# Top-k read without a select pass and without row statistics in its loop; the statistics of 12 batches move to the second cross-attention

## What is computed

```
def top_k_read(query, mem, top_k=32, Wq, bq, Wk, bk, Wv, bv, Wo, bo):   # first block
    q = query @ Wq.T + bq;  k = mem @ Wk.T + bk;  v = mem @ Wv.T + bv
    scores = einsum('btd,bsd->bts', q, k) / sqrt(d)
    keep the 32 largest of the 1601 scores of each row, all others -inf
    attn = softmax(scores);  return (attn @ v) @ Wo.T + bo

def heads_read(q, k, v, norm_w, norm_b, ...):                            # fourth block
    qn = layernorm(q, norm_w, norm_b);  kn = layernorm(k, ...);  vn = layernorm(v, ...)
    Q, K, V = projections of qn, kn, vn into 16 heads of 16
    A = softmax(Q K^T / 4);  O = A V + Q
    return layernorm(O, norm1_w, norm1_b) @ Wo + bo + O

x = x + top_k_read(layernorm(x), ctx, 32, ...)
x = x + retention(layernorm(x), ...)
x = x + mha_and_experts(layernorm(x), ...)
x = x + heads_read(layernorm(x), ctx, ctx, ...)
```

## Time and profile before

| | us |
|---|---|
| median of 3 runs | 1661.69 |
| lowest, highest | 1656.72, 1661.87 |
| the profiled execution | 1658.01 |
| its span | 1656.2 |

### The profile page before, as it was taken

The page is one execution under the profiler, slowest core; times in us unless marked ns, Lnnn a source line. Parts: engine busy times, 40 slices in busy tenths (PEclk is TensorE's granted clock), DMA queues, the critical chain, the costliest instruction groups (busy, mean ns, idle before and its releaser), DMA issues. The chain is left out here.

```text
span 1656.2 us, 29794 instructions
## 1 busy us (share of the span) xinstructions
PE 1468.4 (89%) x11472; PEld 1147.0 (69%) x11472; DVE 994.2 (60%) x1896; ACT 652.8 (39%) x1266; POOL 640.2 (39%) x558
## 2 busy tenths in 40 slices
PE   6988877765993899999999999999999994789998
PEld 3645645444893688888888888888888873456676
DVE  4999954476237456666666665666566643464444
ACT  1444432131201455555555555555455431322322
POOL 0000000001002557877767877677876531311100
PEclk9777788867996999999999999999899965899999
DMA  9479700800322666676676675676674531220000
GB/s 357 145 281 323 264 0 1 296 1 0 104 101 88 172 167 153 163 195 164 153 162 155 159 187 150 157 166 148 164 188 101 112 66 51 80 102 0 1 1 26
DMA packets 109296, 219.61 MB, mean 133 GB/s; under 512 B 10871, under 2 KB 83095, under 8 KB 108391
## 3 DMA queue, kind: packets, MB, share of 16 engines
q1 hardware_dynamic: 109163, 217.80, 47.0%
HBM read 132.51 MB, written 6.40 MB: 84 GB/s over the span
## 5 line engine op out<-in xcount | busy, mean ns | idle before, releaser
L1905 DVE TENSOR_REDUCE d_top<-psum 128x1 f32<-128x400 f32 (+2 forms) x512 | 270.4, 570 | 97.6 <-PE psum L1549 90.4
L1449 POOL TENSOR_TENSOR d_ring<-d_ring 128x512 f32<-128x512 f32 x224 | 289.8, 1294 | 77.0 <-ACT d_ring L1734 59.4
L1734 ACT ACTIVATE d_ring<-psum 128x512 f32<-128x512 f32 (+1 forms) x416 | 229.3, 595 | 206.2 <-PE psum L1567 187.2
L1567 PEld LDWEIGHTS psum<-d_queries,d_stack 100*128 100x128 f32 (+1 forms) x1664 | 214.3, 198 | 36.3 <-issue 33.7
L1567 PE MATMUL psum<-d_queries,d_stack 100*128 100x128 f32 (+1 forms) x1664 | 235.4, 286 | 1.2 <-DVE d_queries L1920 0.9
L1549 PE MATMUL psum<-d_stack,d_queries 96*128 96x400 f32 (+1 forms) x512 | 171.6, 393 | 13.4 <-DVE d_top L1905 10.6
L1379 POOL TENSOR_TENSOR d_rowsT<-d_raw,d_rowsT 128x768 fp32r<-128x768 f32 (+2 forms) x62 | 117.9, 1903 | 154.0 <-ACT d_rowsT L1705 154.0
L1534 PE MATMUL psum<-d_wv,d_rowsT 128*128 128x256 f32 (+1 forms) x1248 | 170.4, 286 | 0.0
L1526 PE MATMUL psum<-d_rowsT,d_wk 128*128 128x384 f32 (+2 forms) x768 | 160.3, 358 | 3.6 <-POOL d_rowsT L1379 1.9
L1534 PEld LDWEIGHTS psum<-d_wv,d_rowsT 128*128 128x128 f32 (+1 forms) x1248 | 161.9, 187 | 0.5 <-issue 0.5
L973 POOL TENSOR_TENSOR c_partL<-moe_in,c_partH 128x256 fp32r<-128x256 f32 x8 | 5.5, 730 | 388.5 <-ACT c_partH L1061 388.5
(11 more groups left out here) (393 smaller groups left out, 2303.0 us busy)
## 6 DMA issues: line engine op xcount, KB each, us to landing
d_stack<-d_stage SPq DMA_DIRECT2D x384, 200.2 KB, 4.2
a_cR<-ctx_rows_dram SPq DMA_DIRECT2D x16, 1664.0 KB, 9.5
a_cT<-ctxT_dram SPq DMA_DIRECT2D x16, 1601.0 KB, 14.5
moe_w<-moe_w_dram SPq DMA_DIRECT2D x16, 1024.0 KB, 11.3
d_rowstd<-row_stds_dram SPq DMA_DIRECT2D x16, 801.0 KB, 5.7
d_raw<-ctxT_dram SPq DMA_DIRECT2D x32, 384.0 KB, 5.7
d_raw<-ctxT_dram SPq DMA_DIRECT2D x16, 512.0 KB, 6.3
d_queries<-queries_dram SPq DMA_DIRECT2D x96, 64.0 KB, 2.0
```

The source lines that it names most:

```text
L1449: pool.tensor_tensor(sums[:, 0, m, :], first, ring[:, slot_of(u, m, c), :], ALU.add)\
L1567: last = pe.matmul(ps[0:w, S_BANK + (m + c) % 2, j * P:(j + 1) * P], stack[0:STACKED, m, j, c * P:c * P + w], queries[0:STACKED, m, j, :], ...
L1734: act.activation(ring[0:w, slot_of(u, m, c), :], ps[0:w, S_BANK + (m + c) % 2, :], ACT.Exp)\
L1905: dve.tensor_reduce(top[:, m, v:v + 1], ps[:, M_BANK + v % 2, 0:min(w, S - s0)], X, ALU.max)\
```

## The change

**In the read.** `TILE` runs through the tiles from 7 down to 0. Tile 7 of x is loaded, normalised and projected first, and the first scores start by quarters of `a_cT`; the other tiles follow in two sets (3 to 6, 0 to 2), in between the first scores. The loops are unrolled. DVE's `choose` has the search alone. ACT takes the exponential of `left` too (what was chosen gives 0), and POOL subtracts: probabilities = exp(scores) - exp(left). The total is the sum over the exponentials of the 32 values found, on ACT. `left`, `probs` and `best` are doubled. For the last tile DVE subtracts. The bias is added to x on POOL at the start. The output projection of tiles 4 to 7 stands before the last two tiles' values. A context row r is now on partition r // 13 (13 rows in one piece per partition, 124 partitions used), so the probabilities are turned from columns 13 apart.

**Row statistics.** None in the loop. `a_cR` still holds batches 0 to 3 at its end: batches 2 and 3 are taken by DVE at the end of the read, 0 and 1 between retention's copies, which stores the four batches' result itself. The other 12 are taken in the second cross-attention: while batch b runs, SP loads the rows of batch b + 4 in two halves into `d_room` (where parameter packs pd1 and, at the end, pd2 lie), DVE takes the statistics in groups 5 and 6 of each half and five small operations at the batch's end, ACT takes Ln and Exp(-0.5 x) in the next batch, and SP stores and loads them again for the rows of that batch.

The core of the diff:

```diff
         @block.gpsimd
         def _(pool):
-            pool.memset(cstats[:, :, :], 0.0).then_inc(sig("a_cleared"), 1)
...
+            for n in range(LAST):
+                pool.wait_ge(sig("a_exp"), n + 1)
+                pool.wait_ge(sig("a_gone"), n + 1)
+                pool.tensor_tensor(probs[:, n % 2, 0:S], probs[:, n % 2, 0:S], left[:, n % 2, :], ALU.subtract)\
+                    .then_inc(sig("a_probs"), 1)
...
# PE
-            score(0, 0, first=True)
-            score(0, 1)
-            value(0, 0, first=True)
-            with pe.Fori(1, NT // 2) as i:
-                score(i, 0)
-                value(i - 1, 1)
-                score(i, 1)
-                value(i, 0)
-            value(NT // 2 - 1, 1)
...
+            turn(2, 4, xn, "a_xnT")
+            score(0)
+            for g in (1, 2):
...
+                project(g, 6, core.w("l0_wqT"), xnT, "a_qT")
...
+                project(g, 4, core.w("l0_wk"), qT, "a_keyqT")
+                bias(g)
+                if g == 1:
+                    score(1)
+            for n in range(1, LAST):
+                score(n + 1)
+                turn_probs(n - 1)
+                value(n - 1)
...
# ACT
+            for n in range(1, NT):
+                exp_left(n - 1)
+                if n >= 2:
+                    take_read(n - 2)
...
+                    gather(n + 1)
+                exp_scores(n)
...
+                take_probs(n - 1)
...
# DVE
-                dve.scalar_tensor_tensor(probs[:, :], left[:, :], LOWEST, probs[:, :], ALU.is_le, ALU.mult,
-                                         accum_out=total[:, u:u + 1]).then_inc(sig("a_probs"), 1)
...
-                    choose(ci, cu)
-                    row_stats(ci, cu)
...
+            for n in range(NT):
+                choose(n)
...
+            row_stats(dve, cR, cstats, 2).then_inc(sig("a_row_stats"), 1)
...
# retention
+            row_stats(dve, cR, cstats, 0, range(0, 9))
...
+                if i < 3:
+                    last = row_stats(dve, cR, cstats, 0, range(9 + 6 * i, min(15 + 6 * i, 2 * NC)))
...
# second cross-attention
+    CONTEXT_AT = {5: (0, 1, 2, 3), 6: (4, 5, 6)}
...
+            def load_context(b, h):
+
+                done = 2 * (b - RESIDENT) + h
...
+                wait(sp, "d_row_stats", done)
+                cs = HALVES_OF[h]
+                sp.dma_start(rows_in[:, 0:cs.stop - cs.start, :],
+                             drams["ctx_rows"][bass.ds(b, 1)].rearrange("b (p c) d -> p (b c) d", c=NC)[:, cs, :])\
+                  .then_inc(sig("d_context_in"), 16)
...
+                act.activation(row_std[:, :], row_var[:, :], ACT.Ln).then_inc(sig("d_row_ln"), 1)
+                act.wait_ge(sig("d_row_ln"), done + 1)
+                act.activation(row_std[:, :], row_std[:, :], ACT.Exp, scale=-0.5).then_inc(sig("d_row_std"), 1)
...
+                    if i in CONTEXT_AT.get(g, ()):
+                        if i == 0:
+                            dve.wait_ge(sig("d_context_in"), 16 * (2 * done + h + 1))
...
+                        last = dve.bn_stats(row_moments[:, c, :], rows_in[:, i, :])
```

More of the change, by code:

```diff
@@ L368, in score @@
+            def score(n):
+                t, u = TILE[n], n % 2
+                projected(pe, "keyqT", set_of(t))
+                if n:
+                    for j in range(2):
+                        pe.wait_ge(sig(f"a_cT_in{u}{j}"), 16 * (n // 2 + u))
                 for c, (s0, w) in enumerate(QUARTERS):
+                    if n:
+                        pe.wait_ge(sig("a_scores"), 4 * (n - 1) + c + 1)
+                    else:
+                        pe.wait_ge(sig(f"a_quarter_in{c}"), 32)
@@ L375, in score @@
                     last.then_inc(sig("a_scores_ps"), 1)
-                if not first:
-                    pe.wait_ge(sig("a_means"), 5 * n)
-                for j in range(2):
-                    for c in range(SHARE):
-                        for k in range(KD):
-                            last = pe.matmul(ps[:, SUM_BANK, j * SHARE + c:j * SHARE + c + 1],
-                                             cT[:, u, j, k, c * P:(c + 1) * P], ones[:, :], start=(k == 0),
-                                             stop=(k == KD - 1))
@@ new lines, in _ @@
+            pe.wait_ge(sig("ident_in"), 16)
+            pe.wait_ge(sig("a_ln_out"), 1)
+            turn(0, 4, xn, "a_xnT")
+            pe.wait_ge(sig("a_pa0_in"), 16)
+            for s, v in both(sig, "a_xnT", 1):
+                pe.wait_ge(s, v)
+            project(0, 6, core.w("l0_wqT"), xnT, "a_qT")
+            projected(pe, "qT", 0)
+            project(0, 4, core.w("l0_wk"), qT, "a_keyqT")
+            bias(0)
+            pe.wait_ge(sig("a_ln_out"), 1 + len(SETS[1]))
+            pe.wait_ge(sig("a_qbk"), 1)
@@ new lines, in _ @@
+            for part, tiles in enumerate((slice(FIRST, NT), slice(0, FIRST))):
+                act.wait_ge(sig("a_var"), part + 1)
+                act.activation(std[:, tiles], var[:, tiles], ACT.Sqrt).then_inc(sig("a_std"), 1)
+                if part == 0:
+                    take(0, 0, 4, xnT, "a_xnT")
+                    act.wait_ge(sig("a_pa0_in"), 16)
+                    take(0, 0, 6, qT, "a_qT", core.p("l0_bq"))
+                    take(0, 0, 4, keyqT, "a_keyqT")
+                    take_bias(0)
@@ new lines, in _ @@
+            take(1, 0, 6, xnT, "a_xnT")
+            take(2, 0, 4, xnT, "a_xnT")
+            gather(0)
+            for k in range(KD):
+                take(1, k, 6, qT, "a_qT", core.p("l0_bq"))
+            exp_scores(0)
+            for k in range(KD):
+                take(1, k, 4, keyqT, "a_keyqT")
+            take_bias(1)
+            for k in range(KD):
+                take(2, k, 6, qT, "a_qT", core.p("l0_bq"))
+            gather(1)
+            for k in range(KD):
+                take(2, k, 4, keyqT, "a_keyqT")
@@ new lines, in _, with row_stats @@
+            dve.tensor_copy(readT[:, 1, 0:HALF], ps[:, 3, :]).then_inc(sig("a_readT_d"), 1)
+            dve.wait_ge(sig("a_valT_ps"), 4)
+            dve.tensor_scalar(valT[:, 1, 0:HALF], ps[:, 5, :], core.p("l0_bv")[:, 1:2], None, ALU.add)\
+               .then_inc(sig("a_valT_d"), 1)
+            for i in range(2, 4):
+                add_out(i, i)
+def row_stats(dve, cR, cstats, first, chunks=range(2 * NC)):
+    for i in chunks:
+        b, c = first + i // NC, i % NC
+        last = dve.bn_stats(cstats[:, b * NC + c, :], cR[:, (NT - 1 - b // 2) % 2, b % 2, c, :])
+    return last
```

628 lines of the change are left out of this document (371 added, 257 removed).

## The result

| kernel | median (lowest to highest), us | runs |
|---|---|---|
| before | 1659.2 (1654.8 to 1661.9) | 4 |
| changed | 1700.8 (1698.9 to 1704.5) | 4 |

The ratio is 1.026, with a 95% interval from 1.023 to 1.029. The forecast was 1601 us with a range from 1580 to 1626; it has the wrong sign. All times here are medians of the fast executions, so one slow execution of experiment 6 (1665.2 us) and one of experiment 7 (1641.1 us) are left out. The profiled execution has a span of 1697.1 us, against 1656.2.

What follows compares the result with a forecast made beforehand. VectorE was taken to bound the read, PE the second cross-attention. The terms -63.7 + 1.5 + 4 = -58.2 gave 1599.8 us from the profiled 1658.0, 1603.5 from the median; 1601 was said, range 1580 to 1626.

Steps and rivals of the forecast that it cites:

- the read: Top-k read: VectorE no longer bounds, tiles follow at 18.45 us, end at 190.5 instead of 254.2 us: minus 63.7.
- Retention: Retention phase: statistics of batches 0 and 1 fit into VectorE's waits, a store ends the phase: plus 1.5 us (0 to 5).
- Second cross-attention ... five small operations (about 1 us) ... plus 4 (0 to 15): Second cross-attention: statistics, small operations, half loads and store for twelve batches, about 0.35 us each: plus 4 us.
- the prediction weighed two others: Read: skill rules of 358 GB/s HBM (18.7 us of transfers a tile) and 16-byte lines (some 3 us more a tile).
- the low part at 855.59: Second cross-attention: VectorE's copy that PE needs at 857.57; seven statistics leave it in time, six and small operations 0.2 us late.
- The slower case: Second cross-attention: VectorE's wait for the half context holds adds and low parts, PE waits; at 3 us a half 1672; 5%.
- The transfer rival: Read: all transfers at 349 GB/s, 19.1 us a tile, read ends at 208, total 1618 us; 6%.
- The clock rivals: Read: slow PE clock, 20.9 us a tile, 1618 us (15%); or fast PE, value 5.8 us, 1588 us (15%).
- Heads cost 1 us a half: Second cross-attention: each half of a batch costs 1 us, 24 us more, total 1622 us; 8%.
- One sign of being wrong: Second cross-attention: the forecast is wrong if that phase takes over 15 us more.
- The one beside it: Heads loop: the forecast is wrong if PE's waits for d_stage or d_stack sum to more than 10 us.
- the signs of being right: Value's ends 18.5 us apart, GpSimd's subtraction near 4, cR at 400 GB/s or more, L2191 without long wait, PE 51.4 of 52.

Runs made afterwards that it cites:

- experiment 6: Changed kernel without the 13 statistics a batch and the half loads in the second cross-attention, small operations kept: 1637.8 us.
- experiment 7: Changed kernel with the five small operations made by GpSimd, at the end of group 1 of the next batch: 1609.9 us.
- experiment 8: Changed kernel with the small operations on VectorE where GpSimd is idle (next batch's second half, end of group 0), statistics double-buffered: 1620.1 us.
- experiment 5: Changed kernel without the five small operations of a batch, Ln reading one column of the statistics directly: 1618.7 us.
- experiment 11: Changed kernel with small operations on VectorE where GpSimd is idle, and five of seven statistics a half one group earlier: 1606.7 us.
- experiment 10: Changed kernel with small operations on GpSimd (end of group 1, next batch) and five of seven statistics a half one group earlier: 1603.4 us.
- experiment 4: Changed kernel without statistics, small operations, Ln, Exp and store in the second cross-attention, half loads kept: 1607.2 us.
- experiment 12: Changed kernel with small operations on GpSimd in its idle stretch (next batch's second half), five of seven statistics a half one group earlier: 1603.1 us.
- 9: Changed kernel with only GpSimd's scaling of raw rows moved, from groups 0, 1, 2 of the first half to 2, 3, 4: 1637.3 us.

## Why the prediction was wrong

**The read and the retention phase: right in the main.** The forecast was -63.7 for the read; measured -57.9. On PE the end of each tile's value (L451) tells where the 5.8 us arose. The first ends at 65.31 us, forecast 60.2. The first search starts at 26.04 (forecast 22.3) and the second at 46.05 (40.4); PE came to score(0) at 19.49 in place of 16.2, having waited 4.61 us for VectorE's normalising of the other seven tiles. The sixth ends at 157.45, forecast 152.5. So the five tiles between took 18.43 us each, and 18.45 was forecast. The pace was right, but not every term of it: three of the tiles take 17.0 to 17.2 us on PE, and the two in which PE waits for cT (3.0 and 2.0 us) take 20.2 and 20.8. VectorE's searches follow each other faster, in 16.7 us in the mean from 46.05 to 146.53, because the first of them started with PE's scores already ahead. The eighth value ends at 184.67 (forecast 183), and the projection and sum behind it take 11.7 us where 7.5 was forecast. Retention: +1.8, forecast +1.5. The phases behind it up to 467 us, forecast 0, cost 3.7 us more; 2.1 of these are one group of 32 matmuls (L221, before L219), which takes 16.09 us at a granted clock of 0.87 in place of 13.97 at 1.00. Where the rest arises was not looked for.

**The step that failed: "Second cross-attention ... five small operations (about 1 us) ... plus 4 (0 to 15)".** It measured 93 us by the spans. Two things were wrong in it.

First the size. "About 1 us" stood there without a row. It is what the five take where GpSimd is idle (0.9 us a batch in experiment 8). They took 53.5 us in 12 batches, 4.5 each time, since operations on VectorE waited for GpSimd's running instruction. The trace of before had such durations, in rows that the forecast read as plain work: one addition of 512 columns takes 0.68 us in one place and 1.67 in another, and three take 2.28 us at 851.72 and 3.26 at the next half's end. The minimum, median and maximum over all 128 say it in one line:

```profile
L1934 DVE TENSOR_TENSOR d_ring<-d_ring x128: 679/692/2127, 586.3 to 1372.2; 128x512 f32<-128x512 f32 x96, 65x512 f32<-65x512 f32 x32
```

```profile
832.18 1.67 DVE L1934 TENSOR_TENSOR d_ring<-d_ring 128x512 f32<-128x512 f32 x1
...
875.49 3.26 DVE L1934 TENSOR_TENSOR d_ring<-d_ring 128x512 f32<-128x512 f32 x3
```

The bounds that the forecast should have had stand in that row: five operations between 5 x 0.17 and 5 x (2.13 - 0.69), so 0.9 to 7 us a batch, up to 86 us in all (an estimate from that row).

The Trainium skill states the mechanism (its page "SBUF — State Buffer", section "Who interferes with whom"): a VectorE instruction with two inputs in SBUF contends with a GpSimd instruction that reads SBUF, and the one that comes second is blocked until the other ends. This case's trace agrees: 1.71 us beside GpSimd's 1.69, 0.17 where GpSimd is idle. By the same section an instruction with at most one such input, outside the modes that use both ports, is spared; the statistics, one input, take 402 to 428 ns in all 156 cases, beside GpSimd or not. The reader who wants a rule that spoke against this change would have found it there; the prediction weighed two others.

Second the wait. The forecast asked when the low part at 855.59 was due. PE needs something earlier: the denominators, which wait for the addition of chunk 12. On the timeline of PE before, at a half's end and at a batch's end:

```profile
856.07 0.62 PE L1595 MATMUL psum<-d_ring,d_ones 128*32 128x128 f32 x16
...
879.85 0.62 PE L1595 MATMUL psum<-d_ring,d_ones 128*32 128x128 f32 x16
```

The additions were done at 854.00 and 878.75: 2.07 us of slack in the middle of a batch and 1.10 at its end. The seven statistics of the first half nearly fit (in the changed kernel PE waits there in the first batch only, 0.93 us). Six statistics and small operations were put at the end with 1.10. So even at 1 us for the five, part of the 3.0 us would have been late; experiment 5, without the small operations, shows that part: 11 us, and 13 come back when the statistics are moved (experiment 11 against 8).

**Waits and clock.** From the first statistics of the second cross-attention to the end PE runs the same 9170 matmuls in both kernels, so the stretch splits by its busy time (columns as in the earlier trace rows; before, then changed):

```profile
519.65:1656.20 1136.55, 1065.84 (x9170) 856.99 (x9170) 660.55 (x1177) 512.22 (x907) 633.28 (x544) 0.93 0.50 125
467.26:1697.10 1229.84, 1100.01 (x9170) 881.99 (x9170) 758.38 (x1393) 519.85 (x931) 621.46 (x544) 0.90 0.51 132
```

PE is idle for 70.7 us before and for 129.8 now: 59.1 of the 93.3 us. The other 34.2 are the same matmuls taking longer, at a granted clock of 0.90 in place of 0.93: after the wait shown above PE works at the lower level for some microseconds, and the same eight score matmuls take 1.97 us at 646.13, behind a wait of 5.50. Experiment 8 has all the work and takes 79.2 us less from that point on, 49.3 of idle time and 29.9 of matmuls. So each microsecond of idle time came with about 0.6 of slower matmuls. The granted clock over the whole span is 0.890 in the changed kernel, 0.914 in experiment 8, 0.923 in the fastest run of experiment 10.

**The rivals.** The slower case had the right sign, and PE did stand behind VectorE's adds, but for another reason: L2191 never waits for the half load, and experiment 4 prices the loads at 8 us. The transfer rival is refuted for the read (433 GB/s). The clock rivals did not come either: PE's clock was 0.84 to 1.00 in the tiles, above the 0.76 and 0.81 of before. "Heads cost 1 us a half" put 24 us on this phase, a quarter of what it cost. With the small operations and the statistics in better places the kernel takes 1603 us. That this is near the 1601 forecast is in part luck: in the profile of experiment 10 the second cross-attention starts 50.4 us earlier than before, where 62.2 was forecast, and what comes from there on takes 9.4 us less, where 4 more was forecast.

**The signs named in advance.** One sign of being wrong came true: the phase takes 93 us more, over the 15. The one beside it named the wrong place: PE's waits for d_stage and d_stack come to 1.2 us, and the 56.3 us are waits for d_ring, which no sign named. Of the signs of being right, value's ends 18.4 us apart, GpSimd's subtraction of 3.0 to 3.6 us, cR above 400 GB/s and L2191 without a wait came; PE at 51.4 of 52 us did not.

## What to carry to other kernels

A tiny instruction is not always a cheap one. Here, operations on 13 columns on VectorE cost the rest of whatever GpSimd was doing. So take the price of such an operation from the maximum in its row, place it where GpSimd is idle, or hand it to GpSimd. When work goes on an engine with "slack", find for each insertion point the next instruction that another engine waits for, and read that slack from the timeline, at every such point of the loop and not at one. If an operation has no row, its bounds decide the range; a price "about 1 us" without a row hid 82 us here.

## What the runs showed of the hardware

- The hold goes both ways: on GpSimd in its own idle stretch (experiment 12), two of the five operations take 0.54 and 0.72 us in the mean, and VectorE's additions run beside them; in experiment 10 none takes over 0.31 in the mean.
- Not only two-operand instructions are held: the TENSOR_SCALAR with one input (L2203) took between 0.17 and 2.09 us, the 2.09 beside GpSimd's scaling of 1024 columns (583.57 and 640.65 us in the changed kernel). The statistics, also with one input, took 402 to 428 ns throughout.
- A transfer with 13 KB per partition reached 433 GB/s from HBM, more than the 422 of cT before.
- After a wait of 3.66 us PE's granted clock was 0.50 to 0.57 for 6.3 us and then 1.00 again.
- How much a kernel scatters from run to run differs: 6 us in the changed kernel, 19 to 22 in experiments 6, 7 and 9, 5 in experiment 8. What makes it was not shown.
